# Linear attention and its FFN on one core: the first block's rows are turned inside the attention's list, and the last tile's norm moves behind the barrier

## What is computed

```python
x = L0_attn_x
x = _layernorm(x + _L0_attn_ref(x, Wq, Wk, Wv, Wo))       # causal linear attention, 16 heads of 16
x = _layernorm(x + _L0_ffn_ref(x, w_gate, w_up, w_down))  # silu(x wg) * (x wu) @ wd, hidden 768
x = _layernorm(x + _L1_attn_ref(x, ...))                  # softmax attention, 8 pairs of heads, difference of two maps
x = _layernorm(x + _L1_ffn_ref(x, ...))                   # two layers of local attention and gated FFN
```

## Time and profile before

| | |
|---|---|
| three runs | 2888.92, 2891.66, 2893.38 us (median 2891.66) |
| the profiled execution, its own time | 2888.54 us |
| its span, first to last instruction | 2886.8 us |
| mean granted TensorE clock | 0.992 of full speed |
| stage a, from start to the first product of stage b | 0 to 262.8 us |
| stage b, to about | 519 us |
| PE, DVE, ACT, POOL busy | 97%, 75%, 57%, 37% |

### The profile page before, as it was taken

One profiled execution on the slowest core, in us unless ns is written; L12 is line 12 of the kernel. 1 busy time (PEld: TensorE's weight loads), 2 busy tenths in 40 slices (PEclk: granted clock), 3 DMA queues, 4 the chain that ended last, 5 costly groups with the idle time before them and its releaser, 6 DMA issues.

```text
span 2886.8 us, 52549 instructions
## 1 busy us (share of the span) xinstructions
PE 2810.2 (97%) x20384; PEld 1890.6 (65%) x20384; DVE 2167.2 (75%) x5059; ACT 1649.1 (57%) x3488; POOL 1054.0 (37%) x1210
## 2 busy tenths in 40 slices
PE   8998999999999999999998899999999999999998
PEld 7777877433333333333334788888888888888887
DVE  7885545778788878877884777777777778888786
ACT  3222332565565656565665676666666766666663
POOL 5343442014112311431232444444445554544442
PEclk9999999999999999999999999999999999999999
DMA  2000010320321222032202100000000100000001
GB/s 80 23 9 23 8 21 4 40 29 6 41 28 18 24 33 25 10 55 23 35 16 74 30 5 5 4 5 4 12 17 29 33 27 5 11 12 12 11 12 61
DMA packets 49149, 66.65 MB, mean 23 GB/s; under 512 B 12590, under 2 KB 37124, under 8 KB 48900
## 3 DMA queue, kind: packets, MB, share of 16 engines
q1 hardware_dynamic: 48900, 63.29, 12.3%
HBM read 24.99 MB, written 8.39 MB: 12 GB/s over the span
## 4 chain that ended last, share of the span: by engine, by line
PE 88%; DVE 5%; ACT 2%; DMA 2%; POOL 1%; issue 1%; SPq 0%; POOLq 0%; ACTq 0%; DVEq 0%
PE ps L1407 17%; PE pw L220 17%; PE ps L220 13%; PE pw L1394 11%; PE ps L1193 6%; PE pw L1193 5%; PE ps L1567 4%; PE pw L1518 3%; PE pw L1480 2%; PE pw L1500 2%; PE ps L1480 1%; PE ps L1518 1%; PE pw L1343 1%; DMA c_qst<-c_mr 1%; PE ps L1343 1%; DVE c_mx L1984 1%
## 5 line engine op out<-in xcount | busy, mean ns | idle before, releaser
L1696 ACT ACTIVATE c_p<-pw 128x512 f32<-128x512 f32 x1024 | 562.3, 595 | 337.5 <-PE ps L1377 178.8
L1407 PE MATMUL ps<-c_p,c_vals 128*64 128x512 f32 x2048 | 546.9, 618 | 3.1 <-ACT c_p L1696 1.9
L1984 DVE TENSOR_REDUCE c_mx<-ps 128x1 f32<-128x512 f32 x694 | 462.4, 683 | 114.3 <-PE ps L1377 104.6
L1394 PEld LDWEIGHTS pw<-c_qst,c_kst 50*128 50x128 f32 x1024 | 154.2, 184 | 366.7 <-ACT c_p L1696 271.8
L1394 PE MATMUL pw<-c_qst,c_kst 50*128 50x512 f32 x1024 | 384.1, 448 | 8.4 <-DMA c_qst<-c_mr 8.0
L1377 PE MATMUL ps<-c_kst,c_qst 48*128 48x512 f32 x694 | 288.9, 451 | 4.5 <-DMA c_kst<-shared 3.5
L1750 ACT ACTIVATE e_sm<-e_sm,e_mx 128x256 f32<-128x256 f32 x512 | 253.8, 499 | 63.7 <-DVE e_mx L2129 63.5
L1984 DVE TENSOR_REDUCE c_mx<-pw 128x1 f32<-128x512 f32 x330 | 225.3, 683 | 46.0 <-PE pw L1377 43.5
L2352 POOL TENSOR_TENSOR e_ss<-e_ss,half 128x16 f32<-128x16 f32 x64 | 186.6, 2915 | 119.6 <-DVE e_ss L2086 105.7
L2249 POOL TENSOR_SCALAR stat<-stat 128x1 f32<-128x1 f32 (+1 forms) x141 | 33.4, 237 | 524.4 <-DVE stat L1856 481.7
L1407 PEld LDWEIGHTS ps<-c_p,c_vals 128*64 128x64 f32 x2048 | 104.3, 135 | 181.7 <-issue 161.6
(11 more groups left out here) (316 smaller groups left out, 6394.1 us busy)
## 6 DMA issues: line engine op xcount, KB each, us to landing
c_kst<-shared SPq DMA_DIRECT2D x192, 64.0 KB
c_qst<-shared SPq DMA_DIRECT2D x64, 128.0 KB
x<-in_L_attn_x SPq DMA_DIRECT2D x8, 512.0 KB, 3.9
c_qst<-shared SPq DMA_DIRECT2D x64, 64.0 KB
keep<-x SPq DMA_DIRECT2D x8, 512.0 KB, 4.0
e_raw<-keep SPq DMA_DIRECT2D x8, 512.0 KB, 3.5
e_hs<-x SPq DMA_DIRECT2D x64, 63.0 KB
out<-x SPq DMA_DIRECT2D x7, 512.0 KB, 5.1
```

The source lines that it names most:

```text
L1394: e.matmul(bank_of("c_s", n, sh, kt, h), c_kst[i][p0:p0 + 50, sh // 2, 128 * kt:128 * kt + 128], c_qst[i][p0:p0 + 50, sh // 2, 512 * h:512 ...
L1407: ins = e.matmul(pv[64 * h:64 * h + 64, :], c_v[:, kt, 33 * hd:33 * hd + 64], p[:, 512 * h:512 * h + 512], start=kt == 0, stop=kt == 7, sk ...
L1696: e.activation(c_p[slot["c_p", (n, sh, kt)]][:, 512 * h:512 * h + 512], bank_of("c_s", n, sh, kt, h), ACT.Exp, scale=0.5).then_inc(SC, 1)
L1984: e.tensor_reduce(c_mx[m % 2][:, qt, h:h + 1], bank_of("c_max", n, sh, qt, h), AX.X, ALU.max).then_inc(VE, 1)
```

## The change

Chunk 31 returns ahead of its norm; the norm's three steps are placed behind `b_begin`. `b_x` of block 0 becomes six steps of stage a's list (PE, ACT and DVE, for each half), due at the time of chunk 31's `a_ot` and 3 later; ACT's waits until the last raw weights are used up, because `b_xb` 0 lies over them. In stage b, block 0 no longer makes `b_x`.

```diff
@@ stage a, chunk(ch)
                 put("dve", "a_wo", after=[("pe", "a_wo", ch)], gives=[(bank, "a_wo", ch)])
+                if ch == NT - 1:
+                    return
                 tile = ("a", ch)
                 op(at(ch, "dve n_st"), "dve", "n_st", tile, 2, ...
@@ stage a, behind the chunks
+            for k in range(2):
+                i, due = (0, k), at(NT - 1, "pe a_ot") + 3 * k
+                op(due, "pe", "b_x", i, 1, [("dve", "n_nm", "a", t) for t in range(4)], [(bank, "b_x", *i)], took=0.44)
+                op(due, "act", "b_x", i, 1, [("pe", "b_x", *i)] + [("pool", "w_out", ("wd", j)) for j in range(2)], took=0.62)
+                op(due, "dve", "b_x", i, 1, [("act", "b_x", *i)], gives=[(bank, "b_x", *i)], took=0.72)
@@ stage b, block(bk)
-                for k in range(2):
+                for k in range(2 if bk else 0):
                     P.use(bank, "dve", "b_x", bk, k, pe=1, act=1, dve=1)
@@ the stages' order
         P.add("b_begin")
+        P.add("n_st", "a", NT - 1, dve=2, pool=2)
+        P.add("n_nm", "a", NT - 1, dve=1)
@@ ACT's b_x(bk, k)
+                for j in range(0 if bk else 2):
+                    w.wait_ge(*pool("w_out", ("wd", j)))
```

## The result

| | before | after |
|---|---|---|
| median, runs on one chip | 2890.03 us (7 runs) | 2881.43 us (7 runs) |
| ratio of the runs, 95% interval | | 0.9967 (0.9955 to 0.9978) |
| profiled execution, own time | 2888.54 us | 2879.46 us |
| its span | 2886.8 us | 2876.6 us |

The changed kernel is faster by 0.33%, some 9.5 us by the ratio (6.4 to 13.0), 8.6 by the medians and 10.2 by the spans of the two profiled executions. 10.9 were forecast. The range on record, 2877.0 to 2886.8, holds the time.

A forecast was written before the change was run, and what follows sets the result against it. PE was taken to bound the kernel, costing twice as much at low clock. 5.5 - 0.6 + 1.6 + 2.8 + 1.6 = 10.9 us less, from 2891.66 to 2880.8 us; range 2877.0 to 2886.8.

The forecast's parts named there:

- The border, 5.5 less 0.6: Stage a to b: `b_g` waits only for DVE's sum of tile 31, 5.5 us less; stage a's last mask 0.6 late.
- The tail: End of stage a: added transposes and subtractions make the last mask 0.6 us late, bounds 0 and 1.7.
- ACT, nothing: ACT at the border: `b_x`'s copies, the raw-weights wait and silu's table load cost nothing.
- It now starts at the barrier: Silu's 1.28 us table load on ACT starts at the barrier, hidden by `b_g`'s 1.4 us.
- The clock at the border, 1.6: PE's clock is kept at stage b's start: first twelve products take 2.75 us, not 4.36; 1.6 us less.
- Rival 1: PE's clock falls at the border all the same; 1.6 us come back, 2882.4 us; chance 0.22.
- The first maximum, 2.8 and 1.6: Stage c's first maximum, one `b_down` and `b_g` later: PE's wait 2.8 us less, kept clock behind it 1.6 less.
- From there on the same shift to the end: From stage c's first maximum on, each step is 10.9 us earlier, to the end.
- rival 4: Slower: later short gaps of PE may lose the clock, 1.6 us per fall; ten more give 2897; chance 0.04.

The follow-up runs named there:

- silu_fill: Changed kernel plus 12 spare transposes in PE's idle border pieces and a tiny Silu ahead of ACT's barrier waits; 2881.68 us, 0.9963 of the kernel before.
- after_again: The changed kernel, unaltered, run and profiled once more; 2881.06 us, 0.9963 of the kernel before.
- fill_border: Changed kernel plus 12 spare transposes filling PE's idle pieces at the border; 2882.09 us, 0.9962 of the kernel before.
- all_edits: Changed kernel plus border filling, early Silu and Exp tables, ones ahead of rotations, later c_lam, third row before fourth stack; 2883.25 us, 0.9967 of the kernel before.
- norm_alone: Kernel before with only the last tile's norm moved behind the barrier; 2889.05 us, 0.9990 of the kernel before.
- banks_undone: Changed kernel with stage b's bank ring begun at bank 2, restoring the banks of the kernel before; 2885.86 us, 0.9984 of the kernel before.

## Why the prediction was right, and where it was not

- **The border, 5.5 less 0.6.** Right: 4.5 for 4.9, the difference of start taken off. `b_g` follows the sum of tile 31 directly and the norm is hidden beside `b_g`. The tail is 0.94 late, not 0.6: chunk 30's masks are 0.87 late, as forecast, but chunk 31's make up nothing of it.
- **ACT, nothing.** Right by luck. "It now starts at the barrier" is wrong: it started behind `b_g`, at 260.65. It cost nothing here since `b_u` at low clock ended at 262.70; with the clock kept it costs 0.5 (silu_fill). The Trainium skill's larger switch cost (ScalarE: Activation LUTs, "What ACT_TABLE_LOAD costs") would have given the same 0.5 from another reason, which the rows do not show: silu starts 0.02 us behind the load's 1.28 here too.
- **The clock at the border, 1.6.** Not in the profiled execution (4.59 for 2.75), there in others. Rival 1 had 0.22; three in six, as measured, would have been the better chance, and the price was too high, because the table load comes up behind the kept clock. By the stretch from `b_g` to `b_down`, 7.32 us before (262.84 to 270.16), the changed kernel gains nothing in its first profile (7.47) and 0.9 in after_again (6.42). This step was mis-sized: 0 or 0.9, not 1.6. With it the sum is 9.3 to 10.2; the ratio gives 9.5.
- **The first maximum, 2.8 and 1.6.** Right, shown by undoing and by doing it alone: 4.3 measured. Two details were off. `b_down` and `b_g` behind the gap took 4.55 us by the lead from 415.44 to 419.99, not about 4.4, so the clock there was worth 1.7. And ACT's ones ending at 405.0 are not all that held the transfer of 409.79: 4.8 us of SP's queue lie between.
- **From there on the same shift to the end.** Not so in the two profiles: the lead is 8.9 at 514, 7.4 at 524, 8.8 at 710, 8.3 at 1247 and 9.7 at 1311 (DVE's `c_rm` before), and 10.15 at the end. Some 1.5 of it comes near 1300, where this execution of the kernel before had a fall of the clock and this one of the changed kernel had none. After_again had none there either, fill_border and all_edits had one. That the end stands so near to the forecast is luck in part. Falls of the clock come and go by the execution, as rival 4 had it, but in both directions, and in after_again 17.2 us less of them were worth 2.2.

## What to carry to other kernels

Read in the order of instructions what an edit moves far from its own place: here a ring of banks that starts at another number was worth about as much as the edit itself, and could be had alone. Count a fall of the clock behind a short gap as open, and price it by what waits next, not by the products alone. Before a gap is closed, look for the queue that its consumers meet later: a lead of 3.6 us at 520 was 0.4 at 544, behind the wait for SP's queue. And before two profiles are compared, see how far apart they stand where their order is still the same.

## What the runs showed of the hardware

- The same program had PE's clock at 0.50 from 259 to 262 in one execution and at 1.00 in another, and 34.2 or 17.0 us of low clock in all, with spans 1.4 us apart. norm_alone kept its clock over a gap of 2.27 us. In banks_undone it fell within the gap of 3.50 us itself (0.51 in the us from 409, with PE idle).
- Where ACT's table load stands: 0.02 us behind a copy when a copy came just before it (262.08), but 0.10 behind the end of what silu waits for when ACT had stood at the barrier (260.65, `b_g` ending at 260.55). Why it differs was not tried; a tiny ACTIVATE of the same function puts it where one wants it.
- A stack of five transfers within SBUF, of 64 or 128 KB each, holds SP's queue for 5.7 to 7.6 us in the first maps of the changed kernel (512 to 555), and a row of two of 4 KB for 1.3 to 2.4.
